# Gates in the queue rows, the residual in memory, and a last stage in 8 pieces: attention and routed experts on one core

## The reference

```
x  = layernorm(x + attention(x))                      # 16 heads of 64, causal
xn = layernorm(x) * gamma + beta
probs = softmax(xn @ router_w.T / 1.5)                # 8 experts
w, idx = top_k(probs, 2)
y_e = silu(xn @ W1[e]) @ W2[e]                        # hidden width 512
out = layernorm(x + w[0] * y_idx0 + w[1] * y_idx1)
```

## Time and profile before

| | us |
|---|---|
| median of 3 runs | 1596.22 |
| lowest, highest | 1593.12, 1596.73 |
| the profiled execution's own time | 1593.55 |
| its span | 1591.8 |
| PE busy | 1445.9 (91% of the span) |
| DVE busy | 1173.1 (74%) |
| ACT busy | 1027.7 (65%) |
| POOL busy | 507.1 (32%) |

### The profile page before, as it was taken

How to read it: one execution, slowest core, us unless ns; L and a number is a source line. 1 busy time by engine, 2 the same in 40 slices (tenths; PEclk the granted TensorE clock), 3 DMA queues, 4 the chain that set the end, 5 groups by cost and what they waited for, 6 DMA issues and landing times.

```text
span 1591.8 us, 32466 instructions
## 1 busy us (share of the span) xinstructions
PE 1445.9 (91%) x10604; PEld 1097.2 (69%) x10604; DVE 1173.1 (74%) x4152; ACT 1027.7 (65%) x3405; POOL 507.1 (32%) x1008
## 2 busy tenths in 40 slices
PE   6999999999999999999999999999954999999900
PEld 4777777777777777777777777777742666666500
DVE  5788888888878888888888888888843555555467
ACT  4777777777777777777777777777732555555424
POOL 1122222233322222223332222223331554555543
PEclk9999999999999999999999999999976999999955
DMA  2000000000000000000000000000005444444255
GB/s 67 7 15 15 15 15 15 15 18 18 18 18 15 15 15 15 15 15 20 20 15 18 15 15 15 15 15 17 20 14 147 146 157 159 161 157 160 89 147 170
DMA packets 87735, 80.18 MB, mean 50 GB/s; under 512 B 10112, under 2 KB 69763, under 8 KB 87568
## 3 DMA queue, kind: packets, MB, share of 16 engines
q1 hardware_dynamic: 77664, 61.08, 12.6%
q0 software_dynamic: 8896, 16.94, 3.2%
q10 hardware_dynamic: 1008, 0.08, 0.0%
HBM read 50.96 MB, written 24.34 MB: 47 GB/s over the span
## 4 chain that ended last, share of the span: by engine, by line
PE 84%; ACT 6%; issue 3%; POOL 2%; DVE 2%; DMA 1%; SPq 1%; POOLq 0%; ACTq 0%; DVEq 0%
PE ps_b L908 13%; PE ps_b L871 13%; PE ps_pt L916 11%; PE ps_a L871 10%; PE ps_s L893 9%; PE ps_s L1047 8%; PE ps_a L1055 8%; PE ps_s L899 5%; PE ps_s L896 3%; ACT probs L557 2%; ACT probs L559 1%; PE ps_pt L921 1%; PE ps_pt L1038 1%; ACT ot L552 1%; PE ps_pt L1064 1%
## 5 line engine op out<-in xcount | busy, mean ns | idle before, releaser
L557 ACT ACTIVATE probs<-ps_s,neg_max 128x256 f32<-128x256 f32 x512 | 242.4, 473 | 33.1 <-DVE neg_max L739 31.2
L432 POOL TENSOR_TENSOR held_pool<-neg_one 128x1 f32<-128x1 f32 x63 | 12.0, 191 | 751.9 <-DVE z L695 751.9
L908 PE MATMUL ps_b<-pt,v 128*64 128x256 f32 (+1 forms) x2048 | 224.2, 340 | 16.0 <-DVE xt_lo L634 12.5
L531 ACT ACTIVATE qk<-ps_a,bq_sb 128x256 f32<-128x256 f32 x256 | 121.3, 474 | 177.5 <-PE ps_a L871 177.3
L916 PE MATMUL ps_pt<-ident,probs 128*128 128x128 f32 x1536 | 223.0, 282 | 0.0
L764 DVE TENSOR_SCALAR probs<-probs,inv_sums 128x256 f32<-128x256 f32 x512 | 207.3, 405 | 18.2
L504 POOL DMA_INDIRECT y_tok<-m_y,m_dest x150 | 147.4, 983 | 171.5 <-DVE m_y L819 77.9
L745 DVE COPY pt<-ps_pt 128x384 f32<-128x384 f32 x256 | 141.8, 554 | 76.9 <-PE ps_pt L916 76.6
L828 DVE SCALAR_TENSOR_TENSOR m_h<-m_tanh,ps_s 128x384 f32<-128x384 f32 x200 | 110.9, 555 | 109.6 <-ACT m_tanh L599 96.2
L552 ACT ACTIVATE ot<-ps_b,bv_sb 128x256 f32<-128x256 f32 x256 | 121.5, 475 | 106.8 <-PE ps_b L908 106.8
L908 PEld LDWEIGHTS ps_b<-pt,v 128*64 128x64 f32 x2048 | 127.7, 136 | 90.1 <-ACT pt L574 26.5
(11 more groups left out here) (153 smaller groups left out, 3009.2 us busy)
## 6 DMA issues: line engine op xcount, KB each, us to landing
m_w<-in_w SPq DMA_DIRECT2D x100, 256.0 KB, 3.1
m_x<-queue SPq DMA_DIRECT2D x50, 195.0 KB, 3.1
f_y<-y_tok SPq DMA_DIRECT2D x32, 256.0 KB, 3.3
x_raw<-in_x SPq DMA_DIRECT2D x32, 128.0 KB, 2.1
x_all<-x_twice SPq DMA_DIRECT2D x32, 128.0 KB, 2.0
out_x<-f_out SPq DMA_DIRECT2D x16, 256.0 KB, 2.4
y_tok<-m_y,m_dest POOLq DMA_INDIRECT x150, 3.0
queue<-z,slot_now POOLq DMA_INDIRECT x128, 2.3
```

The source lines that it names most:

```text
L557: act.activation(probs[:, p % 2, h, 0:2 * P], ps_s[:, p % 2, h, 0:2 * P], ACT.Exp, bias=neg_max[:, h, 0:1], accum_out=sums[:, h, 0:1])
L908: ins = pe.matmul(ps_b[r, dst], v[:, k, q * P + h * DH:q * P + (h + 1) * DH], pt[:, h, src], start=(k == 0), stop=(k == 1), skip_group_che ...
```

## The change

- Queue rows grow from 130 to 132 numbers. VectorE writes the first gate (`GATE`) and the difference of second and first gate (`MORE`) beside `SLOT`, two more instructions for each sequence.
- In the expert stage VectorE works out one gate for each queue row, `MORE` times "this is the second place" plus `GATE`, in two more instructions behind `m_dest`. `rows` multiplies by it while it leaves the accumulator: one copy of 128x384 becomes three `tensor_scalar` of 128x128. SyncE's `load_rows` now waits on `m_gate_done`, not on `m_dest_done`.
- The residual goes to the tensor `x1_tok` in device memory, not to `x1_all`. It comes back to `f_x` in one transfer of 4 MB, 32 KB per partition, issued in expert step 25 behind the weights of step 26. Here token number p*64 + r lies in partition p, not in tile order.
- The last stage has 8 pieces of 8 tiles. Loads and stores are 512 KB each with 4 KB per partition, at a step of 32 KB in memory. VectorE's 16 `scalar_tensor_tensor` of 8 tiles become two plain additions of 128x1024. ACT works in place on `f_x`, which has room for all pieces, so the waits on stored pieces are gone.

```diff
-FIN = 4
+FIN = 8
-    LINE = D + 2
-    TOK, SLOT = D, D + 1
+    LINE = D + 4
+    TOK, SLOT, GATE, MORE = D, D + 1, D + 2, D + 3
...
-                    sp.dma_start(x1_all[:, bass.ds((t - 1) * (TILES * D), TILES * D)],
-                                 x1_twice[:].rearrange("p i d -> p (i d)")).then_inc(x1_stored, 16)
+                    sp.dma_start(x1_tok[(t - 1) * S:t * S].rearrange("(i p) d -> p i d", p=P), x1_twice[:]
+                                 ).then_inc(x1_stored, 16)
...
+                if j == NJ // 2:
+                    sp.wait_ge(x1_stored, SEQS * 16)
+                    sp.dma_start(f_x[:].rearrange("p f d -> p (f d)"), x1_tok.rearrange("(p r) d -> p (r d)", p=P)
+                                 ).then_inc(f_x_loaded, 16)
...
+            y_parts = y_tok.rearrange("(k p f r) d -> k f p (r d)", k=TOP, p=P, f=FINS)
+            out_parts = out.rearrange("s t d -> (s t) d").rearrange("(p f r) d -> f p (r d)", p=P, f=FINS)
...
-                    dve.tensor_copy(z[:, n % 2, :, SLOT], slot_f[:, :, 1]).then_inc(slots_done, 1)
+                    dve.tensor_copy(z[:, n % 2, :, SLOT], slot_f[:, :, 1])
+                    dve.wait_ge(gates_done, t - 1)
+                    dve.tensor_copy(z[:, n % 2, :, GATE], gates[:, :, 0])
+                    dve.tensor_tensor(z[:, n % 2, :, MORE], gates[:, :, 1], gates[:, :, 0], ALU.subtract
+                                      ).then_inc(slots_done, 1)
...
+                dve.tensor_tensor(m_extra[:, j % 2, :], m_second[:, j % 2, :], line[:, :, MORE], ALU.mult
+                                  ).then_inc(m_extra_done, 1)
+                dve.wait_ge(m_extra_done, j + 1)
+                dve.tensor_tensor(m_gate[:, j % 4, :], m_extra[:, j % 2, :], line[:, :, GATE], ALU.add
+                                  ).then_inc(m_gate_done, 1)
...
-                dve.tensor_copy(m_y[:, j % 2].rearrange("p i d -> p (i d)"), ps_pt[:, 1, 0:ROWS]
-                                ).then_inc(m_rows_done, 1)
+                dve.wait_ge(m_gate_done, j + 1)
+                for i in range(BLOCKS):
+                    ins = dve.tensor_scalar(m_y[:, j % 2, i, :], ps_pt[:, 1, i * P:(i + 1) * P],
+                                            m_gate[:, j % 4, i:i + 1], None, ALU.mult)
+                ins.then_inc(m_rows_done, 1)
...
+                dve.tensor_tensor(f_y[:, buf, 0, :], f_y[:, buf, 0, :], f_y[:, buf, 1, :], ALU.add
+                                  ).then_inc(f_first_done, 1)
+                dve.wait_ge(f_first_done, f + 1)
+                dve.tensor_tensor(f_x[:, f, :], f_x[:, f, :], f_y[:, buf, 0, :], ALU.add).then_inc(f_res_done, 1)
```

More of the change, by code:

```diff
@@ L170, in postln_block @@
         m_dest = sb("m_dest", [P, 4, BLOCKS], I32)
-        f_y = sb("f_y", [P, 3, FIN, TOP, D])
-        f_res = sb("f_res", [P, 2, FIN, D])
+        m_extra = sb("m_extra", [P, 2, BLOCKS])
+        m_gate = sb("m_gate", [P, 4, BLOCKS])
+        f_y = sb("f_y", [P, 3, TOP, FIN * D])
+        f_x = sb("f_x", [P, FINS, FIN * D])
         f_stats = sb("f_stats", [P, FIN, 6])
@@ L240, in postln_block @@
         slots_done = sem("slots_done")
+        gates_done = sem("gates_done")
         xb_done = sem("xb_done")
@@ L262, in postln_block @@
         m_dest_done = sem("m_dest_done")
+        m_extra_done = sem("m_extra_done")
+        m_gate_done = sem("m_gate_done")
         m_y_sent = [sem("m_y_sent_even"), sem("m_y_sent_odd")]
         f_y_loaded = [sem("f_y_loaded_%d" % i) for i in range(3)]
+        f_x_loaded = sem("f_x_loaded")
         f_first_done = sem("f_first_done")
@@ L375, in load_y @@
                 for k in range(TOP):
-                    first = k * TOKENS + f * FIN * P
-                    sp.dma_start(f_y[:, f % 3, :, k, :], y_tok[first:first + FIN * P].rearrange("(i p) d -> p i d", p=P)
-                                 ).then_inc(f_y_loaded[f % 3], 16)
+                    sp.dma_start(f_y[:, f % 3, k, :], y_parts[k, f]).then_inc(f_y_loaded[f % 3], 16)
             load_y(0)
             load_y(1)
-            out_rows = out.rearrange("s (i p) d -> p (s i) d", p=P)
             for f in range(FINS):
@@ L386, in _ @@
                 sp.wait_ge(f_out_done, f + 1)
-                sp.dma_start(out_rows[:, f * FIN:(f + 1) * FIN, :], f_out[:, f % 2]
-                             ).then_inc(f_out_stored[f % 2], 16)
-            for par in range(2):
-                sp.wait_ge(f_out_stored[par], FINS // 2 * 16)
+                sp.dma_start(out_parts[f], f_x[:, f, :]).then_inc(f_out_stored, 16)
+            sp.wait_ge(f_out_stored, FINS * 16)
         @block.gpsimd
@@ L608, in _ @@
                 act.wait_ge(f_shift_done, f + 1)
-                if f >= 2:
-                    act.wait_ge(f_out_stored[f % 2], f // 2 * 16)
                 for i in range(FIN):
-                    ins = act.activation(f_out[:, f % 2, i, :], f_res[:, f % 2, i, :], ACT.Identity,
+                    cols = slice(i * D, (i + 1) * D)
+                    ins = act.activation(f_x[:, f, cols], f_x[:, f, cols], ACT.Identity,
                                          scale=f_r[:, f % 2, i:i + 1], bias=f_shift[:, f % 2, i:i + 1])
@@ L656, in small_parts @@
                     dve.scalar_tensor_tensor(
-                        out=gate_all[:, bass.ds((t - 2) * (TILES * TOP), TILES * TOP)].rearrange(
-                            "p (i k) -> p i k", i=TILES),
-                        in0=r_top[:, :, 0:TOP], scalar=0.5,
-                        in1=r_inv[:].unsqueeze(2).to_broadcast([P, TILES, TOP]), op0=ALU.mult, op1=ALU.mult)
+                        out=gates[:], in0=r_top[:, :, 0:TOP], scalar=0.5,
+                        in1=r_inv[:].unsqueeze(2).to_broadcast([P, TILES, TOP]), op0=ALU.mult, op1=ALU.mult
+                        ).then_inc(gates_done, 1)
                     dve.wait_ge(r_idxf_done, t - 1)
@@ L804, in destinations @@
                 dve.wait_ge(m_x_loaded[j % WBUFS], (j // WBUFS + 1) * 16)
-                dve.scalar_tensor_tensor(out=m_second[:, j % 2, :], in0=m_x[:, j % WBUFS, :, SLOT],
-                                         scalar=t_row[:, j:j + 1], in1=row_no[:], op0=ALU.subtract,
-                                         op1=ALU.is_equal).then_inc(m_second_done, 1)
+                line = m_x[:, j % WBUFS]
+                dve.scalar_tensor_tensor(out=m_second[:, j % 2, :], in0=line[:, :, SLOT], scalar=t_row[:, j:j + 1],
+                                         in1=row_no[:], op0=ALU.subtract, op1=ALU.is_equal
+                                         ).then_inc(m_second_done, 1)
                 dve.wait_ge(m_second_done, j + 1)
@@ L834, in _ @@
             rows(NJ - 1)
[L836 removed]
+            dve.wait_ge(f_x_loaded, 16)
             for f in range(FINS):
```

41 lines of the change are left out of this document (12 added, 29 removed).

## The result

| | before | changed |
|---|---|---|
| median of six runs each, us | 1595.46 | 1583.58 |
| lowest, highest | 1593.12, 1597.37 | 1581.97, 1589.07 |
| profiled execution's own time | 1593.55 | 1589.07 |
| its span | 1591.8 | 1587.3 |

What follows compares the result with a forecast made beforehand. PE was taken to bound the expert stage, a loop of waits the last stage. Last stage -15.6, expert work +0.2, residual load +2.5, attention +0.3 sum to -12.6 us: forecast 1583 us, range 1575 to 1591.

Steps and rivals of the forecast that it cites:

- What bounds the last stage: Last stage: a loop of waits over stores and loads stays the bound, 16.4 us for three pieces against VectorE's 14.4.
- The prediction's figure for VectorE alone: Last stage: 52.2 us, -19.6, if VectorE alone set the pace; held impossible at any rate seen.
- The last stage's size: Last stage, first load's issue to the end of the span: 56.2 us against 71.8, so -15.6.
- the power in it took 0.717 us for 2 columns and 1.006 for 4, so about 1.6 for 8: 2.7 in all: Last stage, from VectorE's last statistics to ACT: 2.7 us a piece, 2.11 before, scaled from GpSimd's power on fewer columns.
- the 380 GB/s between store and next piece: Last stage: 1.57 MB in a store and loads take 4.14 us at 380 GB/s plus 1.55 fixed, 5.7 in all.
- The slow bound: Last stage with transfers at only 284 GB/s: 60.4 us, a gain of 11.4.
- The queue: Expert stage: the residual's 4.19 MB load in SyncE's queue delays weights PE needs; +2.5 us, bounds 0 to 8.5.
- rival 3: Last stage and residual load: strided reads run slowly; at 190 GB/s the kernel takes 1607 us; chance 0.05.
- The rule on row pitches: Device memory layout: copies fall at large power-of-two pitches, 207 GB/s at 512 KiB to 103 at 4 MiB; 32 KB unlisted.
- nearly in time: Expert stage: scatters land nearly in time beside the residual's load, as DMA engines alternate queues by packet; 1.4 us slack.
- The new work per step: Expert stage, VectorE: gate instructions and three copies add 0.6 us per step, hidden in 2.06; +0.2 at the end.
- Rival 4: Expert stage: VectorE becomes the step's bound; at 2.5 us more per step it costs 22, giving 1603 us; chance 0.03.

Runs made afterwards that it cites:

- load first: Changed kernel with SyncE asking for piece f+3 before it waits for and stores piece f: 1576.53 us, 0.9884 of the kernel before; repeated on another chip, 1579.26 us, 0.9832.

## Why the prediction was right, and where it was wrong

- **What bounds the last stage: right.** The loop over the stores stayed the bound, shown by load first (63.0 to 52.4). The prediction's figure for VectorE alone, 52.2, is what load first measured (52.4).
- **The last stage's size: wrong, -8.5 instead of -15.6.** The parts of the miss, by the first trace: first load +0.5 (5.1, not 4.6). Piece to store, in both loops, +1.6 and +1.7 (12.3 and 12.5, not 10.75). Store to next piece +0.8 and +1.2. Piece 6 to 7 +1.7 (6.5, not 4.8, its load queued behind a store and other loads). The rest, from piece 7's start to the end of the span, -0.4. Sum +7.1.
- **The step that failed first** is "the power in it took 0.717 us for 2 columns and 1.006 for 4, so about 1.6 for 8: 2.7 in all". The 1.6 was right for GpSimd alone (1.64). But no term stood for the long additions that hold GpSimd up: 0.9 us each on `f_negmean` and on the power. The earlier trace rows could not show it, since VectorE's work beside GpSimd in the kernel before did not hold it up.
- **The step that failed second** is the 380 GB/s between store and next piece. Loads alone beat it, the mix of loads and a store did not reach it. 1.57 MB in 6.46 less 1.55 fixed is 320 GB/s, and 296 in the second loop. Part of it is that the next piece's store enters the same queue (1546.18) while piece 3's loads are still on their way, which the term left out. This is read from windows and timeline; no run isolates the store.
- **The slow bound failed too.** -11.4 was called the end of the range, since 284 GB/s seemed the worst; it left GpSimd's term fixed. The range held only by the total.
- **The queue: right in kind, half the size in the changed kernel.** The load cost 1.2 and 1.5 us in its two traces (+2.5 forecast, within its bounds 0 to 8.5), and nothing in eight parts. That the stage as a whole came to +2.3 in the first trace is partly the longer first step, which differs by 1.0 us between the two traces of the changed kernel. In all seven traces the load cost 1.0 to 4.4 us, since two waits of 0 to 2 us each and the clock behind them decide. The waits for scatters and for weights fell in two steps, where the prediction had them overlap. By the packets in the trace the 4 MB moved from 1363.3 to 1375.3, 12 us as forecast; the 32 KB pieces took 1.2 us each, and all transfers together ran at 392 GB/s from 1370 to 1375, so rival 3 is out. The rule on row pitches that the prediction quotes from the Trainium skill does not show at 32 KB: 416 GB/s in loads.
- **Scatters were held up more than "nearly in time"**: 8.8 us to landing at the most, where 3.4 is the median. The slack of 1.4 was used up, and 0.3 us passed on to TensorE.
- **The new work per step: right.** Each step hides it (5.82 us as before); on the way out it costs 0.3 instead of 0.2. Rival 4 is out.
- **The total: right partly by luck.** The traces give -4.5 and -9.1 us. The medians give -11.9. By the traces what varies most is ahead of the experts, where the prediction has +0.3, where the two traces of the changed kernel differ by 3.6 us, and where attention can differ by 10 us between two traces of one kernel. Of the executions without a trace the stages are not known, so it is not shown where the missing 7 us were made up.

## What to carry to other kernels

When a queue issues loads and stores of one loop, ask for the next load before waiting for the work that the store needs; here that gave 10.6 us in the stage (8.0 in the median of the launch), more than the rewrite of the stage gave without it (8.5 to 8.8). Price a small instruction by what its neighbours on other engines do at that moment, since long additions on VectorE held up the GpSimd instructions that started inside them until they had ended. A large transfer in a queue that also feeds the critical engine was better split here, though the engines had room on average.

## What was not expected of the hardware

GpSimd's power of 128x8 took 1.64 us alone and 2.50 to 2.53 beside a 128x1024 addition on VectorE. A row of four `scalar_tensor_tensor` of 128x128 held it for 0.15 us at most, a row of eight plain additions of 128x128 for 1.4. Attention in the same kernel took 10 us longer on one chip than on another, with waits of 0.5 us for ScalarE that the shorter course does not have. TensorE ran at its lower clock after a wait of 2.06 us but not after 1.68. Six loads of 512 KB in rows of 512 B occupied SyncE for 8.4 us, in rows of 4 KB for 2.9.
